# A non-local attention block in fp32: from image 3 on, theta, phi and their weights' remainders share one matmul

## The reference

```python
theta = x @ W_theta                    # 1024 x 32
phi   = maxpool2x2(x @ W_phi)          # 256 x 32
g     = maxpool2x2(x @ W_g)            # 256 x 128
beta  = softmax(theta @ phi.T)         # 1024 x 256
y     = gamma * (beta @ g) @ W_o + x   # 1024 x 256
```

## Time and profile before

| | |
|---|---|
| median of 3 runs | 239.31 us (239.09 to 239.55) |
| time of the profiled execution | 239.57 us |
| its span, first to last instruction | 237.7 us |
| busy: TensorE matmul / VectorE / GpSimd / ScalarE | 98% / 86% / 70% / 62% |

### The profile page before, as it was taken

One profiled execution on the slowest core, in us unless ns is written; L12 is line 12 of the kernel. 1 busy time (PEld: TensorE's weight loads), 2 busy tenths in 40 slices (PEclk: granted clock), 3 DMA queues, 4 the chain that ended last, 5 costly groups with the idle time before them and its releaser, 6 DMA issues.

```text
span 237.7 us, 4361 instructions
## 1 busy us (share of the span) xinstructions
PE 232.0 (98%) x1464; PEld 207.8 (87%) x1464; DVE 205.3 (86%) x475; ACT 147.8 (62%) x274; POOL 167.3 (70%) x119
## 2 busy tenths in 40 slices
PE   7999999999999999999999999999999999999994
PEld 4777888988989899898989989898998989989794
DVE  5699988989888898988989899898988989899785
ACT  3665948577483866838477492847748385645640
POOL 1488698868679686768867677786867868642870
PEclk9999999999999999999999999999999999999999
DMA  7693029396592937739194683928659293725854
GB/s 238 220 365 128 3 70 337 130 272 258 119 374 88 337 151 242 292 105 382 60 327 191 194 341 108 343 85 289 241 150 383 61 338 139 247 107 190 318 204 181
DMA packets 14934, 51.14 MB, mean 215 GB/s; under 512 B 1856, under 2 KB 2496, under 8 KB 14912
## 3 DMA queue, kind: packets, MB, share of 16 engines
q1 hardware_dynamic: 14512, 50.67, 60.6%
q10 hardware_dynamic: 400, 0.20, 0.3%
HBM read 33.95 MB, written 16.78 MB: 213 GB/s over the span
## 4 chain that ended last, share of the span: by engine, by line
PE 89%; DMA 5%; DVE 4%; issue 1%; ACT 1%; SPq 0%; DVEq 0%
PE proj L209 23%; PE out L350 18%; PE proj L216 12%; PE proj L350 8%; PE score L255 6%; PE shift L350 6%; PE shift L310 5%; PE score L350 4%; PE score L282 4%; DMA x_t<-in_xt 2%; DMA out<-y_sb 2%; PE shift L209 1%; DVE y_sb L669 1%; DVE neg_parts L643 1%; PE score L265 1%; PE out L282 1%
## 5 line engine op out<-in xcount | busy, mean ns | idle before, releaser
L564 POOL TENSOR_TENSOR e_lo<-e_sb,e_hi 128x512 fp32r<-128x512 f32 x64 | 82.0, 1294 | 45.7 <-ACT e_sb L488 45.7
L559 POOL TENSOR_TENSOR x_lo<-x_t,x_hi 128x1024 fp32r<-128x1024 f32 x30 | 71.8, 2399 | 8.7 <-ACT x_hi L444 8.7
L485 ACT ACTIVATE e_hi<-shift 128x512 fp32r<-128x512 f32 x60 | 36.0, 600 | 17.9 <-PE shift L310 17.0
L209 PE MATMUL proj<-x_hi,w_hi 128*128 128x512 f32 x118 | 46.8, 397 | 0.1
L209 PE MATMUL proj<-x_hi,w_lo 128*128 128x512 f32 x118 | 46.6, 395 | 0.0
L643 DVE TENSOR_REDUCE neg_parts<-score 128x2 f32<-128x512 f32 x64 | 43.6, 686 | 1.1 <-PE score L255 0.2
L350 PE MATMUL out<-G_lo,e_hi 128*128 128x258 f32 x132 | 37.4, 284 | 0.0
L350 PE MATMUL out<-G_hi,e_hi 128*128 128x258 f32 x132 | 37.4, 283 | 0.0
L216 PE MATMUL proj<-x_lo,w_hi 128*128 128x512 f32 x118 | 37.3, 396 | 0.0
L350 PE MATMUL out<-G_hi,e_lo 128*128 128x258 f32 x132 | 37.2, 282 | 0.0
L488 ACT ACTIVATE e_sb<-shift 128x512 f32<-128x512 f32 x60 | 36.1, 602 | 0.0
(11 more groups left out here) (107 smaller groups left out, 480.8 us busy)
## 6 DMA issues: line engine op xcount, KB each, us to landing
x_t<-in_xt SPq DMA_DIRECT2D x32, 512.0 KB, 5.2
x_n<-in_xn SPq DMA_DIRECT2D x32, 512.0 KB, 7.6
out<-y_sb SPq DMA_DIRECT2D x31, 512.0 KB, 6.2
w_sb<-in_w_proj SPq DMA_DIRECT2D x1, 256.0 KB, 2.8
theta<-neg_hi ACTq DMA_DIRECT2D x16, 4.0 KB
theta<-neg_lo SPq DMA_DIRECT2D x16, 4.0 KB
out<-y_sb SPq DMA_DIRECT2D x1, 256.0 KB, 2.1
wo_sb<-in_w_out SPq DMA_DIRECT2D x1, 128.5 KB, 5.7
```

Source lines behind the costliest of these rows:

```text
L209: nc.tensor.matmul(bank_[:, :], w[:, c, cols:cols + P], x_hi[:, i % 2, h, c, :], start=(c == 0 and n == 0), stop=False)
L485: nc.scalar.activation(e_hi[:, i % 2, n, :], shift_bank(i, n)[:, :], ACT.Exp)
L559: nc.gpsimd.tensor_tensor(x_lo[:, i % 2, h], x_t[:, i % 2, h], x_hi[:, i % 2, h].bitcast(f32), ALU.subtract).then_inc(x_lo_ready, 1)
L564: nc.gpsimd.tensor_tensor(e_lo[:, i % 2, n, :], e_sb[:, n, :], e_hi[:, i % 2, n, :].bitcast(f32), ALU.subtract).then_inc(e_lo_ready, 1)
```

## The change

- `pair_hi` multiplies `x_hi` by `w_pair`, whose 128 columns are [w_hi of theta and phi | w_lo of theta and phi]. Rows 0 to 63 of `proj[h]` get the leading product and rows 64 to 127 the correction. `pair_lo` adds `x_lo` times the first 64 columns. `copy_corr` (ScalarE) copies rows 64 to 127 to `corr`, and `add_corr` adds them to rows 0 to 63 by one matmul of 512 columns with a unit matrix (`lower`); rows 0 to 63 of `corr` are zero.
- Theta is now there once. `theta_high` copies 32 rows, and a DMA (`twin`, on SP's queue) copies them to rows 64 to 95 of the stack. The pooled phi goes to `proj[0]`, rows 64 to 95.
- GpSimd makes `w_pair`, `lower` and the zeros of `corr` once, after `w_og` and before its first `x_low`.
- The values go to `outb[0]` and `outb[1]`, the outputs' banks change, and the orders of all engines with them. turn_max(b) stands after two outputs instead of three, from stage 2 on.

```diff
+        def phi_max(i):
+            return outb[1][THETA:P, 0:NK] if i < PACK else proj[0][PAIR:THETA, 0:NK]
         def value_bank(i, h):
-            return shift[h] if i < 2 else proj[h]
+            return shift[h] if i < 2 else proj[h] if i == 2 else outb[h]
...
+            if i == 0:
+                return (outb[0], outb[1], shift[0], shift[1], outb[0], outb[1], outb[0], outb[1])[t]
+            if i < LAST - 2:
+                return (outb[0], proj[1], shift[0], outb[1], proj[0], score[1], outb[0], outb[1])[t]
...
@@ sync @@
+            def twin(i, h):
+                pixels = slice(HALF * h, HALF * (h + 1))
+                sp.wait_ge(theta_hi_ready, 2 * i + h + 1)
+                sp.dma_start(theta[2 * DK:THETA, i % 3, pixels].bitcast(f32),
+                             theta[0:DK, i % 3, pixels].bitcast(f32)).then_inc(theta_twin[i % 3][h], 16)
...
@@ tensor @@
+            def pair_hi(i, h):
...
+                for c in range(CC):
+                    last = nc.tensor.matmul(proj[h][:, :], w_pair[:, c, :], x_hi[:, i % 2, h, c, :],
+                                            start=(c == 0), stop=(c == CC - 1), skip_group_check=True)
+                last.then_inc(corr_ready, 1)
+
+            def pair_lo(i, h):
+                pe.wait_ge(x_lo_ready, 2 * i + h + 1)
+                for c in range(CC):
+                    nc.tensor.matmul(proj[h][0:PAIR, :], w_pair[:, c, 0:PAIR], x_lo[:, i % 2, h, c, :],
+                                     start=False, stop=False, skip_group_check=True)
...
+            def add_corr(i, h):
...
+                pe.wait_ge(corr_copied, packed(i, h))
+                nc.tensor.matmul(proj[h][0:PAIR, :], lower[:, :], corr[:, h, :],
+                                 start=False, stop=True, skip_group_check=True).then_inc(tp_ready, 1)
...
@@ tensor: output(i, t) @@
+                elif t == 0:
+                    pe.wait_ge(g_pooled, 2 * later + 1)
...
@@ tensor: the loop @@
                 if s > 2:
-                    for h in range(2):
-                        theta_phi(a, h)
-                        scores(b, h)
-                        shifted(d, 2 + h)
-                    for h in range(2):
-                        values(a, h)
-                        scores(b, 2 + h)
+                    pair(a, 0)
+                    scores(b, 0)
+                    shifted(d, 2)
+                    add_corr(a, 0)
+                    pair(a, 1)
+                    scores(b, 1)
+                    shifted(d, 3)
+                    scores(b, 2)
+                    add_corr(a, 1)
+                    values(a, 0)
+                    scores(b, 3)
+                    values(a, 1)
                 if a < LAST:
-                    outputs(d, (0, 1, 2))
+                    outputs(d, (0, 1))
                     turn_max(b)
-                    outputs(d, (3, 4))
+                    outputs(d, (2, 3, 4))
                     mix(a)
-                    outputs(d, (5, 6))
+                    output(d, 5)
                     shifted(b, 0)
                     shifted(b, 1)
-                    output(d, 7)
+                    outputs(d, (6, 7))
...
@@ scalar: the loop @@
-                    for h in range(2):
-                        theta_high(a, h)
-                        exps(d, 2 + h)
+                    copy_corr(a, 0)
+                    theta_high(a, 0)
+                    copy_corr(a, 1)
+                    exps(d, 2)
+                    theta_high(a, 1)
+                    exps(d, 3)
                     phi_high(a)
...
@@ vector: the loop @@
                 if s > 2:
-                    for h in range(2):
-                        phi_pool(a, h)
-                        theta_low(a, h)
-                        maxima(b, h)
-                    phi_low(a)
+                    maxima(b, 0)
+                    phi_pool(a, 0)
+                    theta_low(a, 0)
+                    maxima(b, 1)
+                    phi_pool(a, 1)
+                    theta_low(a, 1)
+                    maxima(b, 2)
                     g_pool(a, 0)
-                    maxima(b, 2)
+                    maxima(b, 3)
                     if a < LAST:
                         g_pool(a, 1)
-                    maxima(b, 3)
+                    phi_low(a)
```

More of the change, by code:

```diff
@@ L19 @@
 GW = C + 2
+PAIR = 2 * DK
 PROJ = P + DV
+PACK = 3
 WARM = 8
@@ L78, in out_bank @@
         def out_bank(i, t):
+            if i == 0:
+                return (outb[0], outb[1], shift[0], shift[1], outb[0], outb[1], outb[0], outb[1])[t]
+            if i < LAST - 2:
+                return (outb[0], proj[1], shift[0], outb[1], proj[0], score[1], outb[0], outb[1])[t]
             if i == LAST - 2:
[L80 to L83, removed]
+                return (outb[0], proj[1], proj[0])[t % 3]
+            return proj[0] if i < LAST and t == 0 else (shift[1], outb[0], outb[1], shift[0])[t % 4]
         def shift_bank(i, n):
@@ L122, in neg_loads, with twins, packed @@
             return 32 * (i // 3 + 1)
+        def twins(i):
+            return 16 * (i // 3)
+        def packed(i, h):
+            return 2 * (i - PACK) + h + 1
         def max_row(i, r):
@@ L163, in _ @@
                 a, b, d = s, s - 1, s - 2
+                if a >= PACK:
+                    for h in range(2):
+                        twin(a, h)
                 max_into_stack(b)
@@ L171, in _ @@
                 store(d, 1)
+            for h in range(2):
+                twin(LAST, h)
             max_into_stack(LAST - 1)
@@ L231, in values, with pair @@
                     pe.wait_ge(g_pooled, h + 1)
-                elif i > 1:
+                elif i == 2:
                     pe.wait_ge(theta_lo_ready, 2 * i + h + 1)
                     pe.wait_ge(phi_pooled, 2 * i + h + 1)
+                elif i > 2:
+                    pe.wait_ge(y_ready, TILES * (i - 3) + 7 + h)
                 project(i, h, P, value_bank(i, h), g_ready)
-            def scores(i, n):
+            def pair_hi(i, h):
+                if i == PACK:
+                    if h == 0:
+                        pe.wait_ge(w_pair_ready, 2)
+                    pe.wait_ge(g_pooled, 2 * (i - 1) + h + 1)
+                else:
+                    pe.wait_ge(y_ready, TILES * (i - 3) + (5 if h == 0 else 2))
+                pe.wait_ge(x_hi_ready, 2 * i + h)
+                for c in range(CC):
[7 more added lines that the diff above has]
+                                     start=False, stop=False, skip_group_check=True)
+            def pair(i, h):
+                pair_hi(i, h)
+                pair_lo(i, h)
+            def add_corr(i, h):
+                if i == PACK and h == 0:
+                    pe.wait_ge(lower_ready, 1)
+                    pe.wait_ge(corr_zero, 1)
+                pe.wait_ge(corr_copied, packed(i, h))
+                nc.tensor.matmul(proj[h][0:PAIR, :], lower[:, :], corr[:, h, :],
+                                 start=False, stop=True, skip_group_check=True).then_inc(tp_ready, 1)
+            def scores(i, n):
+                h = n // 2
+                if n in (0, 2):
+                    pe.wait_ge(theta_lo_ready, 2 * i + h + 1)
+                    if i >= PACK:
+                        pe.wait_ge(theta_twin[i % 3][h], twins(i))
                 if n == 0:
-                    pe.wait_ge(theta_lo_ready, 2 * i + 2)
                     pe.wait_ge(phi_hi_ready, 2 * i + 2)
@@ L336, in output @@
                 elif t == 4:
[L337 to L339 removed]
+                    pe.wait_ge(phi_hi_ready, 2 * later + 2)
+                    pe.wait_ge(phi_lo_ready, later + 1)
+                elif t == 5:
+                    pe.wait_ge(neg_lo_ready, i + 2)
                 else:
[L341 removed]
+                    pe.wait_ge(y_ready, TILES * i + (1 if t == 6 else 4))
@@ L451, in theta_high, with copy_corr @@
                 act.wait_ge(tp_ready, 2 * i + h + 1)
-                nc.scalar.copy(theta[0:THETA, i % 3, HALF * h:HALF * (h + 1)],
-                               proj[h][0:THETA, :]).then_inc(theta_hi_ready, 1)
+                rows = slice(0, THETA if i < PACK else DK)
+                nc.scalar.copy(theta[rows, i % 3, HALF * h:HALF * (h + 1)],
+                               proj[h][rows, :]).then_inc(theta_hi_ready, 1)
+            def copy_corr(i, h):
+                act.wait_ge(corr_ready, packed(i, h))
+                nc.scalar.copy(corr[PAIR:P, h, :], proj[h][PAIR:P, :]).then_inc(corr_copied, 1)
             def phi_high(i):
                 act.wait_ge(phi_pooled, 2 * i + 2)
-                nc.scalar.copy(phi[0:DK, i % 3, :], phi_max).then_inc(phi_hi_ready, 1)
+                nc.scalar.copy(phi[0:DK, i % 3, :], phi_max(i)).then_inc(phi_hi_ready, 1)
                 act.wait_ge(phi_hi_ready, 2 * i + 1)
@@ L590, in _ @@
                 e_low(d, 3)
-                if a == 2:
+                if a < LAST:
                     g_low(a)
                     x_low(a + 1, 0)
-                    x_low(a + 1, 1)
-                elif a < LAST:
```

(4 more changed lines are left out.)

95 lines of the change are left out of this document (59 added, 36 removed).

## The result

The changed kernel takes 243.33 us (median of 4 runs, 243.13 to 245.76) against 239.43 us before (4 runs, 239.09 to 241.11): 1.0172 times as long, 95% interval 1.0092 to 1.0252. A second measurement on another chip gave 243.22 against 239.48, 1.0157 [1.0125, 1.0190]. The profiled execution took 243.13 us, its span 241.0 us, 3.3 more than before. The forecast was 241.7 in a range of 238.7 to 246.6, slower. Ratios are taken over fast executions; the slow ones, of which the longest is a single one of 457 us in filler, are not in them.

What follows compares the result with a forecast made beforehand. TensorE sets the pace, with VectorE some 0.7 us slack per stage. 239.57 + 1.4 (wait before output 0) + 0.2 (first x_low) + 0.7 (stage 2's turn_max) = 241.9, about 241.7 against the median; range 238.7 to 246.6.

Steps and rivals of the forecast that it cites:

- the likeliest case: The whole kernel: slower, 241.7 us, with its own range of 240.3 to 243.3; chance 0.62.
- TensorE's own saving: Each theta_phi half: five matmuls instead of six, 0.467 us less per stage; part before the first output 6.54 us.
- The new wait: Output 0 waits for g_pool(a,0), eighth on VectorE, ending at 7.01; stage 14.21 us, 0.11 more; +1.4 us in all.
- restart term: TensorE's first two matmuls after a wait on VectorE lose 0.11 us, so output 0 begins in effect at 7.12.
- The inputs in time: Inputs of VectorE's eight instructions arrive in time: add_corr slips at most 0.1, theta_low's input has 0.3 us to spare.
- The start: GpSimd's added setup makes x_low 0.4 us late, 0.2 taken; stage 2's moved turn_max(1) adds 0.72 us.
- turn_max(1)'s part: Stage 2: turn_max(1) still waits for the fourth maxima, with one more output behind it: +0.72 us.
- The end: From stage 15's output 0 to the end: no term in the sum, taken as unchanged.
- 1: Rival: VectorE's chain to g_pool(a,0) falls to 6.4 us, under TensorE's 6.54, so TensorE is dense: 234.1 us; chance 0.1.
- 2: Rival: only theta_low's two gaps to maxima on VectorE close, 0.22 us less per stage: 238.8 us; chance 0.1.
- 3: Rival: phi_pool reading and writing proj[0] is slower by 0.18 us, twice per stage: +4.7, 246.3 us; chance 0.12.
- 4: Rival: eight changes per stage between 128 and 64 columns drain TensorE's array, +0.89 us per stage: 251.8 us; chance 0.06.

Runs made afterwards that it cites:

- filler: The changed kernel with two more 512-column matmuls per stage from stage 3 on, ahead of values(a,1), results overwritten: 243.03 us, 1.0117 of the kernel before.
- gpool_first: The changed kernel with g_pool(a,0) moved ahead of maxima(b,2) on VectorE: 236.68 us, 0.9861 of the kernel before.
- the padded kernels: The changed kernel, without and with three reorderings, with 34 warming matmuls of 120 columns in place of 8 of 512: 246.50 and 237.97 us.
- all_three: The changed kernel with g_pool(a,0) before maxima(b,2), stage 2's turn_max(1) behind three outputs, scores(b,0) between pair_hi and pair_lo: 235.47 us, 0.9829 of the kernel before.
- all_three_last_buffer: all_three plus an own buffer for the last image's second half, so its finishes skip the wait for a store: 233.73 us, 0.9746 of the kernel before.
- gpool_first_filler: The changed kernel with g_pool(a,0) before maxima(b,2) and two more 512-column matmuls ahead of values(a,1) per stage: 240.15 us, 1.0026 of the kernel before.
- all_three_padded: all_three with 34 warming matmuls of 120 columns at the very start in place of 8 of 512: 237.97 us, 0.9915 of the kernel before.

## Why the prediction was right, and where its sizes were off

The direction and the mechanism came true; the 243.33 lies at the upper edge of the 240.3 to 243.3 that was given to the likeliest case. That it is no further off is in part luck: two terms were too small or missing, and one too large took 0.45 of it back.

**TensorE's own saving: right.** Five matmuls a half, pitch 0.233, the part before output 0 6.53 us when nothing holds it (125.45 - 118.92 in gpool_first) for a forecast of 6.54. The stage without the wait is 13.64.

**The new wait: right, to the hundredth, as far as VectorE goes.** Counted from the stage's start at 122.14, maxima(b,0) starts at 1.38 (forecast 1.37), the six distances from there to maxima(b,2) are 0.73, 0.73, 0.71, 0.72, 0.73 and 0.72 (4.34; forecast 4.36), g_pool follows after 0.61, and its end is at 7.01 (forecast 7.01). The runs bear out the mechanism from both sides: g_pool(a,0) moved up takes 0.6 away, two matmuls more on TensorE add nothing. Its **restart term was too small**: 0.11 from the earlier trace rows, whose first matmul came 0.03 after the release. Here it is 0.10 (129.15 to 129.25) and another 0.07 to the second one, 0.17 in all. A stage is 14.26, not 14.21; over 13 stages the profile has 2.12 us for the 1.43 (13 x 0.11) of the prediction, 0.7 more. Why this restart takes 0.07 more than that of the earlier trace rows is open.

**The inputs in time: right.** No wait in a stage but the one; add_corr is in its place at 1.41 (forecast 1.40), and the twins hold nobody.

**The start: 0.45 for a forecast of 0.9.** GpSimd's additions took 0.95, 0.31, 0.29 and 0.28, overlap by some hundredths, and fit into the gap that was there; x_low starts at 10.26, before it was 10.27. The 0.2 for it was nothing. turn_max(1)'s part, from stage 2's output 0 to stage 3, was 0.64 for a forecast of 0.72.

```profile
8.60 0.95 POOL L667 MEMSET corr<- 64x1024 f32 x1
9.50 0.31 POOL L669 CAST lower<-ident 128x64 fp32r<-128x64 f32 x1
...
10.26 4.75 POOL L652 TENSOR_TENSOR x_lo<-x_t,x_hi 128x1024 fp32r<-128x1024 f32 x2
```

**The end: not in the sum, +0.73.** The prediction treated the tail as unchanged because its work is. But a finish there already waited 0.18 us for a store, and the 26 matmuls that went moved an instruction load into that store's time. The wait became 1.74, 1.56 more; the rest of the end is 0.83 shorter, of which 0.51 is TensorE's wait of the earlier trace rows, which is not there any more. That the load's date keeps step with TensorE's count is shown by the counts and by the padded kernels; that what it loads is TensorE's own program is inferred from them.

Together: +0.7 for the restart, +0.7 for the end and -0.45 for the start are some +1.0; another 0.26 lies outside the span, which grew by 3.3 where the time of the profiled execution grew by 3.56. That is the 1.2 by which its 243.13 lies above the sum's 241.9. The medians (243.33 for a forecast of 241.7) are 1.6 apart; the remaining 0.4 is between executions.

**The rivals.** 1 and 2 fell: phi_pool and theta_low kept their distances although theta_low reads from row 0. 3 fell: phi_pool in place takes 0.70, distance 0.73 (0.71 and 0.75 before). The prediction has 246.3 for it in one place and 246.6 as the range's upper end: 241.9 + 4.7, without the 0.26 taken off. 4 fell: eight changes between 128 and 64 columns in a stage cost nothing, 6.53 us for 28 units. The rule that a change of tiling mode drains TensorE (the Trainium skill, TensorEngine Tiling (Array Packing), Key Properties) therefore doesn't show in matmuls of fp32r that only narrow the stationary side to 64.

**Open.** One stage that is longer than the others (13.94 and 13.93 in gpool_first and all_three, 14.86 and 14.9 in all_three_last_buffer and gpool_first_filler, 13.91 twice in all_three_padded) appears only in kernels with g_pool(a,0) moved up, not always at the same place. In each of them the time is lost in front of shifted(b,0), and where the profile names a releaser it is neg_lo's DMA:

```profile
62.58 0.73 PE L375 MATMUL shift<-theta,phi 98*128 98x512 f32 x2 [0.97 <-DMA theta<-neg_lo]
```

The same DMA is why the end still differs where nobody waits for the store (26.02 against 25.13: a wait of 1.22 against 0.20). It also differs between the two executions of the changed kernel (0 and 0.78). Why this small DMA comes late in some stages no run shows. That would be the next place to look.

## To carry to other kernels

Taking work from the busiest engine helps only if every wait that the new layout brings is met in the shorter time: place each one in the other engine's order and add its distances up from the last thing that can hold it. If the sum lies above the shortened work, first try the order on that other engine; exchanging two instructions turned 1.7% slower into 1.4% faster. And look for waits that are barely met or already last a tenth or two, the tail included: a change that touches nothing there can lengthen them.

## What the runs showed of the hardware

- A load of instructions (one packet, 0.02 MB, 0.93 us in the changed kernel's profile and up to 1.8 in others) holds one of the 16 DMA engines, and the share of a 512 KB store that is on that engine waits: the store lands after 4.4 to 5.2 us instead of 2.6 to 3.1. 26 matmuls fewer on TensorE were enough to bring it there.
- A matmul's restart after a wait on VectorE cost 0.17 us here, 0.10 to the first and 0.07 to the second, where another place in the same kernel had 0.03 and 0.08.
- At the very start, 34 matmuls of 120 columns took 7.51 us, 0.22 each, and 8 of 512 columns 3.78, 0.47 each: as many columns in short pieces cost twice the time, at a granted clock of 1.00 both times. Later 258 columns cost 0.12 and 512 cost 0.233.
- On VectorE two neighbours of 128 rows overlapped, 0.60 from start to start, and around the ones of 32 rows it was 0.71 to 0.73, for the same duration of 0.68 to 0.70. Whether the number of rows or the row at which they start decides, no run separates.
